# The combine of a mixture-of-experts layer: sums from accumulators, squares on ScalarE, a new order of the pass, four shared-expert groups early

## The chip, the cores and the metric

One Trainium2 chip, one core of it. The time is that of the whole kernel on the device in microseconds, a median over runs. "A change within measurement" means about 0.2% here.

## What is computed

An attention layer with random features, then a layer with 32 routed experts (four per token, at most 512 tokens each) and one shared expert; both are wrapped in `x + layernorm(f(layernorm(x)))`. The change touches the end of the second:

```python
ye = jnp.einsum('eci,eid->ecd', h, W2)                 # routed experts
yrows = ye[eid, posc] * gflat[:, None]
out = yrows.reshape(-1, K, D).sum(axis=1)
out = out + jax.nn.silu(X @ sw1.T) * (X @ sw3.T) @ sw2.T   # shared expert
x = x + _layernorm(out)          # (out - mean) / sqrt(var + 1e-5)
```

There are T = 8192 tokens of E = 512 numbers; float32 outside of the matmuls.

## The kernel before

Three stretches matter. First, routing ends: GpSimd scatters token slots to DRAM (`send`, L1260), one indirect DMA per 128 choices. Meanwhile the shared expert runs for NS = 2 groups *early* (`up`, `down`, `silu`, `make_high`, `hidden`, `low`, `copy_early`), and their result is stored to the accumulator `acc` in DRAM (`store_early`, L1564). Then slots are loaded, the rows of expert 0 gathered (L1412), turned on TensorE (`turn`, L1462) and the 32 experts run. Each adds its weighted rows to `acc` by an indirect DMA of GpSimd (L1426).

Last comes the combine, 16 passes `q` over the groups in ORDER. A *heavy* pass has a group whose shared expert was not early: it forms `up` of the next group and `down` of this one. A *light* pass (groups under NS) has no shared expert left. In each heavy pass:

- TensorE: `up` of the next group, 32 matmuls 128x512 (L1485), `down` of this one, 4 x 4 matmuls (L1500) into two banks `ys`, of which the third and fourth `down` wait until `include` has read the first and second.
- ScalarE: `silu` of the next group's two halves (L1540), `make_high` (L1546, the rounded half of `h`), `scale` of the pass before (L1552, four instructions with a scale and a bias per partition: the layernorm), `store` (L1559, a DMA issue).
- VectorE: `make_shift` (L1663, 128x4), `hidden` (L1610), `low` (L1615), `include` (L1642: `acc` block plus `ys`), `measure` (L1651, bn_stats of a block), `add` (L1670: the residual, 2048 wide), `aggregate` (L1656).
- GpSimd: `make_rstd`, variance plus epsilon (L1436) and its power -0.5 (L1438), between `aggregate` and `make_shift`.
- SP: `load_acc` (L1361; five buffers `total`), `load_shared` (L1348, the turned groups; eight buffers), `load_x1` (L1354; five buffers, a new load waits for the store that frees it).

A single `stats`, `mv`, `rstd` and `shift` serve all passes. ScalarE's table for silu is loaded once before the first `silu`.

## Time and profile before

| | us |
|---|---|
| median of 3 runs | 2089.63 (2088.13 to 2090.12) |
| the profiled execution, whole | 2089.07 |
| its span, first to last instruction | 2087.3 |
| TensorE busy | 1819.7 (87%) |
| VectorE busy | 1207.8 (58%) |
| ScalarE busy | 1124.8 (54%) |
| GpSimd busy | 758.3 (36%) |

All times within the trace are counted from the start of the span. Shares of the span are averages over stages with different limits, so the stretches have to be read one by one. The granted clock is TensorE's, as a share of full speed.

### The profile page before, as it was taken

What the parts mean: (1) busy time and instruction counts of PE and PEld (TensorE: products, weight loads), DVE (VectorE), ACT (ScalarE), POOL (GpSimd) and SP (SyncE); (2) the same over time, 40 slices, a digit from 0 to 9 for tenths busy, and PEclk for the clock granted to TensorE, in tenths of its full rate; (3) what the DMA queues carried; (4) which work ended last, traced back from release to release, by engine and by line L of the source; (5) the groups of instructions that cost most, each with busy time, mean ns of one, the idle gap of its engine ahead of it and who ended that gap; (6) DMA issues with size and microseconds to landing.
All of it is one profiled execution on the core that took longest, in us unless ns stands there. A gap on an engine that the chain in (4) does not pass through costs nothing.

```text
span 2087.3 us, 33721 instructions
## 1 busy us (share of the span) xinstructions
PE 1819.7 (87%) x12976; PEld 889.0 (43%) x12976; DVE 1207.8 (58%) x2230; ACT 1124.8 (54%) x1371; POOL 758.3 (36%) x718
## 2 busy tenths in 40 slices
PE   8999999999969998897888887455999989987795
PEld 5444444444448785132333333222444444443331
DVE  6776767676620000376888898861444344445786
ACT  5565555555436665586778775513444444432443
POOL 0000000000000000015877787874777777761110
PEclk9999999999979999999999999777999999999997
DMA  7445444446368885768877775342999999987983
GB/s 249 165 137 184 143 177 143 178 139 212 107 173 211 211 212 133 171 206 180 244 220 222 230 221 186 137 171 79 203 206 234 242 241 241 202 147 243 344 292 129
DMA packets 188848, 405.15 MB, mean 194 GB/s; under 512 B 33812, under 2 KB 72084, under 8 KB 172064
## 3 DMA queue, kind: packets, MB, share of 16 engines
q1 hardware_dynamic: 83184, 222.41, 35.6%
q10 hardware_dynamic: 68640, 124.26, 17.3%
q0 software_dynamic: 36864, 56.32, 14.4%
q8 instruction: 103, 1.69, 0.3%
q14 instruction: 57, 0.47, 0.1%
HBM read 237.06 MB, written 177.08 MB: 198 GB/s over the span
## 4 chain that ended last, share of the span: by engine, by line
PE 13%; DMA 12%; DVE 12%; issue 10%; POOL 9%; ACT 4%; SPq 1%; POOLq 0%; DVEq 0%; ACTq 0%
POOL slot_dram L1260 4%; DMA acc_dram<-s_y,s_slot 3%; PE s_gates L1485 3%; PE s_ups L1485 3%; PE s_ys L1500 2%; DMA s_spread<-share_dram 2%; DMA s_rows<-rows_dram,s_slot 2%; POOL acc_dram L1426 2%; DMA den_dram<-s_den 2%; PE s_turned L1462 1%; DVE s_stats L1651 1%; ACT s_xT L1531 1%; DVE s_x L1670 1%; POOL s_rows L1412 1%; PE s_y L898 1%
## 5 line engine op out<-in xcount | busy, mean ns | idle before, releaser
L258 PE MATMUL s_proj<-s_xT,keep_wqkv 128*128 128x512 f16 x1536 | 341.8, 379 | 0.0
L1260 POOL DMA_INDIRECT slot_dram<-keep_filled,keep_slots x256 | 292.1, 1141 | 105.2 <-issue 74.4
L1426 POOL DMA_INDIRECT acc_dram<-s_y,s_slot x128 | 205.1, 1603 | 93.0 <-issue 35.6
L258 PEld LDWEIGHTS s_proj<-s_xT,keep_wqkv 128*128 128x128 f16 x1536 | 147.8, 98 | 183.2 <-issue 12.6
L898 PE MATMUL s_y<-keep_wo,s_at_hl 128*128 128x512 f16 x768 | 188.6, 398 | 36.9 <-ACT s_z L988 36.9
L1540 ACT ACTIVATE s_gate<-s_gates 128x512 f32<-128x512 f32 x96 | 57.1, 597 | 263.8 <-PE s_ups L1485 218.4
L1610 DVE SCALAR_TENSOR_TENSOR s_h<-s_gate,s_ups 128x512 f32<-128x512 f32 x96 | 65.9, 686 | 216.1 <-ACT s_gate L1540 216.1
L339 POOL TENSOR_SCALAR s_rstd<-s_mv 128x4 f32<-128x4 f32 x16 | 16.0, 998 | 458.9 <-DVE s_mv L354 458.9
L676 ACT ACTIVATE s_phi<-s_logits 128x1024 f32<-128x1024 f32 x128 | 131.1, 1024 | 83.9 <-PE s_logits L697 83.9
L237 PE MATMUL s_proj<-keep_wqkv,s_xT 128*128 128x512 f16 x768 | 173.8, 383 | 1.2 <-ACT s_xT L500 1.2
L967 ACT ACTIVATE s_phi<-s_logits 128x1024 f32<-128x1024 f32 x128 | 131.4, 1027 | 63.5 <-PE s_logits L867 62.6
L518 ACT ACTIVATE s_hl<-s_rot 128x1024 f16<-128x1024 f32 x64 | 67.6, 1057 | 179.0 <-DVE s_rot L400 169.9
L387 DVE TENSOR_TENSOR s_by_cos<-s_proj,s_table 128x1024 f32<-128x1024 f32 x64 | 78.3, 1224 | 133.6 <-PE s_proj L258 133.6
L1531 ACT ACTIVATE s_xT<-s_turned 128x1024 f16<-128x1024 f16 x128 | 125.5, 1019 | 44.5 <-PE s_turned L1462 44.2
L1412 POOL DMA_INDIRECT s_rows<-rows_dram,s_slot x128 | 132.7, 1037 | 42.7 <-issue 30.8
L898 PEld LDWEIGHTS s_y<-keep_wo,s_at_hl 128*128 128x128 f16 x768 | 72.7, 101 | 170.6 <-issue 55.7
L737 PE MATMUL s_parts<-s_phi,s_v 128*33 128x128 f32 x2048 | 137.9, 277 | 2.3 <-DMA s_v<-v_dram 2.2
L1500 PE MATMUL s_ys<-s_w,s_parts 128*128 128x512 bf16 x512 | 132.1, 382 | 3.5 <-DVE s_y L1627 3.5
L1485 PE MATMUL s_gates<-s_xT,s_w 128*128 128x512 f16 x512 | 124.3, 387 | 10.4 <-ACT s_xT L1531 10.4
L1485 PE MATMUL s_ups<-s_xT,s_w 128*128 128x512 f16 x512 | 122.1, 382 | 0.0
L1627 DVE TENSOR_SCALAR s_y<-s_ys,s_slot 128x512 f32<-128x512 f32 x128 | 93.9, 748 | 43.8 <-PE s_ys L1500 43.6
L1462 PE MATMUL s_turned<-keep_ident,s_rows 128*128 128x128 f16 x1024 | 80.3, 223 | 44.6 <-DMA s_rows<-rows_dram,s_slot 35.0
(165 smaller groups left out, 3202.8 us busy)
## 6 DMA issues: line engine op xcount, KB each, us to landing
s_x<-x_in SPq DMA_DIRECT2D x32, 1024.0 KB, 11.9
qk_dram<-s_hl ACTq DMA_DIRECT2D x32, 1024.0 KB, 6.0
keep_ahead<-qk_dram SPq DMA_DIRECT2D x48, 512.0 KB
acc_dram<-s_zero SPq DMA_DIRECT2D x17, 1024.0 KB, 13.9
v_dram<-s_v ACTq DMA_DIRECT2D x16, 1056.0 KB, 6.9
s_v<-v_dram SPq DMA_DIRECT2D x16, 1056.0 KB, 11.2
s_spread<-share_dram SPq DMA_DIRECT2D x64, 256.0 KB
x_dram<-s_x ACTq DMA_DIRECT2D x16, 1024.0 KB, 5.6
```

The lines of the kernel that those rows point to most:

```text
L237: mm = nc.tensor.matmul(proj[half][:, 512 * b:512 * b + 512], left, right, start=(c == 0 and i == 0), stop=(c == EC - 1 and i == 2))
L258: mm = nc.tensor.matmul(out[:, 512 * b:512 * b + 512], left, right, start=(c == 0 and i == 0), stop=(c == EC - 1 and i == 2))
L676: nc.scalar.activation(phi[n % 2][:].rearrange("p h m -> p (h m)"), logits[n % 2][:], ACT.Exp, scale=1.0 / M_SCALE).then_inc(phi_ready, 1)
L737: mm = nc.tensor.matmul(parts[ch % 2][at:at + D + 1, h // 2 * M:(h // 2 + 1) * M], v[n % 2][:, a * H + h, :], phi[half][:, h % HALF, :], s ...
L898: mm = nc.tensor.matmul(y[m % 2][:], at_hl[n % 2][:, s, c, a * P:(a + 1) * P], keep["wo"][:, w, c, :], start=(c == 0 and i == 0), stop=(c ...
L967: nc.scalar.activation(phi[m % PHIS][:].rearrange("p h q -> p (h q)"), logits[:], ACT.Exp, scale=1.0 / M_SCALE).then_inc(phi_ready, 1)
L1260: nc.gpsimd.indirect_dma_start(out=io["slot"], out_offset=bass.IndirectOffsetOnAxis(ap=slots[n % 2][:, a * K + j:a * K + j + 1], axis=0), ...
L1412: nc.gpsimd.indirect_dma_start(out=rows[r][:, a, :], out_offset=None, in_=io["rows"], in_offset=bass.IndirectOffsetOnAxis(ap=slot[e % RING ...
L1426: nc.gpsimd.indirect_dma_start(out=io["acc"], out_offset=bass.IndirectOffsetOnAxis(ap=slot[e % RING][:, a, 0:1], axis=0), in_=y[e % 2][:, ...
L1485: mm = nc.tensor.matmul(bank[:], w[:, c, i * P:(i + 1) * P], left[:, s, c, :], start=(c == 0 and s == 0), stop=(c == EC - 1 and s == 1))
L1500: mm = nc.tensor.matmul(ys[a % 2][:], parts[p % 2][:, i, s, a * P:(a + 1) * P], w[:, i, :], start=(i == 0 and s == 0), stop=(i == IC - 1 a ...
L1531: nc.scalar.activation(xT[k][:, :, :, a * P:(a + 1) * P], turned[a % 2][:].bitcast(F16).rearrange("p (s c q) -> p s c q", s=2, c=EC), ACT. ...
```

## The change

NS becomes 4: four shared-expert groups run early, and four of the combine's passes are light. `include` writes out the sum of each row with its result (`accum_out`), so `measure` and `aggregate` go; in a light pass `sum_up` does it, adding a tile of zeros that a memset sets once. `center` makes minus the mean, scaled; ScalarE's `square` forms the sum of the squares of the centred block, which is the variance. The small tiles become pairs, so that passes wait two back instead of one. ScalarE's order in a pass is now `square`, `silu` 0, `make_high` 0, `store` of two passes back, `scale`, `silu` 1, `make_high` 1. VectorE's is `hidden` 0, `make_shift`, `low` 0, `include` 0 and 1, `hidden` 1, `include` 2 and 3, `center`, `low` 1, `add`.

```diff
-        NS = 2
+        NS = 4
-        ORDER = (2, 3, 4, 0, 5, 6, 7, 1, 8, 9, 10, 11, 12, 13, 14, 15)
+        ORDER = (4, 5, 0, 6, 7, 1, 8, 9, 2, 10, 11, 3, 12, 13, 14, 15)
...
+        sums, centre, var, rstd, shift = (t.pair(n, [P, A]) for n in ("sums", "centre", "var", "rstd", "shift"))
+        squares = xT[0][:].rearrange("p s c q -> p (s c q)").bitcast(F32).rearrange("p (a e) -> p a e", a=A)
+        nothing = w13[0][:].rearrange("p w c i -> p (w c i)").bitcast(F32)[:, 0:E]
...
+            def make_rstd(q):
+                k = q % 2
+                pool.wait_ge(squared, q + 1)
+                if q >= 2:
+                    pool.wait_ge(z_ready, q - 1)
+                nc.gpsimd.tensor_scalar(rstd[k][:], var[k][:], 1e-5, None, ALU.add).then_inc(var_ready, 1)
...
+            def square(q):
+                k = q % 2
+                act.wait_ge(centre_ready, q + 1)
+                for a in range(A):
+                    ins = nc.scalar.activation(squares[:, a, :], total[q % ACCS][:, a, :], ACT.Square,
+                                               bias=centre[k][:, a:a + 1], scale=E ** -0.5,
+                                               accum_out=var[k][:, a:a + 1])
+                ins.then_inc(squared, 1)
...
+                if q >= 1:
+                    square(q - 1)
                 if more:
-                    for i in range(IC):
-                        silu(p + 1, i)
+                    silu(p + 1, 0)
                     make_high(p + 1, 0)
+                if q >= 2:
+                    store(q - 2)
                 if q >= 1:
                     scale(q - 1)
                 if more:
+                    silu(p + 1, 1)
                     make_high(p + 1, 1)
-                if q >= 1:
-                    store(q - 1)
+            square(NG - 1)
+            store(NG - 2)
             scale(NG - 1)
             store(NG - 1)
...
                 nc.vector.scalar_tensor_tensor(out=at, in0=ys[a % 2][:], scalar=1.0 / H_SCALE, in1=at, op0=ALU.mult,
-                                               op1=ALU.add).then_inc(y_copied, 1)
+                                               op1=ALU.add, accum_out=sums[q % 2][:, a:a + 1]).then_inc(y_copied, 1)
+
+            def sum_up(q, a):
...
+                nc.vector.scalar_tensor_tensor(out=at, in0=at, scalar=1.0, in1=nothing, op0=ALU.mult, op1=ALU.add,
+                                               accum_out=sums[q % 2][:, a:a + 1]).then_inc(summed, 1)
+
+            def center(q):
...
+                nc.vector.tensor_scalar(centre[k][:], sums[k][:], -E ** -1.5, None, ALU.mult).then_inc(centre_ready, 1)
...
+            nc.vector.memset(nothing, 0.0).then_inc(nothing_set, 1)
+            dve.wait_ge(nothing_set, 1)
             for q, n in enumerate(ORDER):
                 p = NE + n
+                more = n >= NS and p + 1 < PASSES
+                if more:
+                    hidden(p + 1, 0)
                 if q >= 1:
                     make_shift(q - 1)
+                if more:
+                    low(p + 1, 0)
                 if n >= NS:
...
                     include(q, 0)
+                    include(q, 1)
                     if more:
                         hidden(p + 1, 1)
...
                     include(q, 2)
...
                     include(q, 3)
...
+                        sum_up(q, a)
+                center(q)
+                if more:
+                    low(p + 1, 1)
+                if q >= 1:
                     add(q - 1)
-                aggregate(q)
             make_shift(NG - 1)
             add(NG - 1)
```

## Rows read from the trace of the kernel before

**Rows 1.** The page: busy us (share of the span) and instructions of each engine.
```profile
PE 1819.7 (87%) x12976; PEld 889.0 (43%) x12976; DVE 1207.8 (58%) x2230; ACT 1124.8 (54%) x1371; POOL 758.3 (36%) x718
```

**Rows 2.** Busy time by stretch: us, then PE, PEld, DVE, ACT, POOL, PEclk, DMA, GB/s.
```profile
1898.00:2087.00 189.00, 142.65 (x600) 57.96 (x600) 147.57 (x267) 73.76 (x113) 20.23 (x32) 0.88 0.73 265
...
1932.00:1952.00 20.00, 12.79 (x53) 5.13 (x52) 15.36 (x32) 8.58 (x13) 3.40 (x6) 0.83 0.99 369
```

**Rows 3.** Timeline of a heavy pass: start, us, engine, line, operation, count, [idle before, releaser].
```profile
2042.14 0.16 DVE L1663 SCALAR_TENSOR_TENSOR s_shift<-s_mv,s_rstd 128x4 f32<-128x4 f32 x1 [1.47 <-POOL s_rstd L1438]
2042.25 0.69 DVE L1610 SCALAR_TENSOR_TENSOR s_h<-s_gate,s_ups 128x512 f32<-128x512 f32 x1
2042.86 0.68 DVE L1642 SCALAR_TENSOR_TENSOR s_rows<-s_ys,s_rows 128x512 f32<-128x512 f32 x1
2042.97 0.63 ACT L1546 ACTIVATE s_parts<-s_h 128x512 f16<-128x512 f32 x1 [0.46 <-DVE s_h L1610]
...
2043.51 2.92 ACT L1552 ACTIVATE s_rows<-s_rows,s_shift,s_rstd 128x512 f32<-128x512 f32 x4
...
2048.83 2.28 DVE L1670 TENSOR_TENSOR s_x<-s_x,s_rows 128x2048 f32<-128x2048 f32 x1
...
2051.14 0.38 ACTq L1559 DMA_DIRECT2D out_dram<-s_x  x1
...
2051.62 0.60 ACT L1540 ACTIVATE s_gate<-s_gates 128x512 f32<-128x512 f32 x1 [4.68 <-DVE s_x L1670]
2051.75 0.38 DVE L1656 BATCH_NORM_AGGREGATE s_mv<-s_stats 128x2 f32<-128x6 f32 x4
...
2053.60 0.16 DVE L1663 SCALAR_TENSOR_TENSOR s_shift<-s_mv,s_rstd 128x4 f32<-128x4 f32 x1 [1.47 <-POOL s_rstd L1438]
```

**Rows 4.** Timeline of a light pass and of TensorE's first matmuls behind it.
```profile
1975.96 0.16 DVE L1663 SCALAR_TENSOR_TENSOR s_shift<-s_mv,s_rstd 128x4 f32<-128x4 f32 x1 [1.47 <-POOL s_rstd L1438]
...
1983.18 0.16 DVE L1663 SCALAR_TENSOR_TENSOR s_shift<-s_mv,s_rstd 128x4 f32<-128x4 f32 x1 [1.47 <-POOL s_rstd L1438]
...
1984.63 3.67 PE L1500 MATMUL s_ys<-s_sw,s_parts 128*128 128x512 bf16 x8 [7.21 <-DVE s_rows L1642]
```

**Rows 5.** Timeline of the combine's first two passes, and the last shift.
```profile
1898.22 0.69 DVE L1642 SCALAR_TENSOR_TENSOR s_y<-s_ys,s_y 128x512 f32<-128x512 f32 x1 [12.87 <-DMA s_y<-acc_dram]
...
1911.55 0.69 DVE L1642 SCALAR_TENSOR_TENSOR s_y<-s_ys,s_y 128x512 f32<-128x512 f32 x1 [3.07 <-PE s_ys L1500]
...
1922.29 0.16 DVE L1663 SCALAR_TENSOR_TENSOR s_shift<-s_mv,s_rstd 128x4 f32<-128x4 f32 x1 [1.47 <-POOL s_rstd L1438]
...
2074.96 0.16 DVE L1663 SCALAR_TENSOR_TENSOR s_shift<-s_mv,s_rstd 128x4 f32<-128x4 f32 x1 [1.47 <-POOL s_rstd L1438]
```

**Rows 6.** Timeline of TensorE between the routing and the first expert.
```profile
1397.50 1.89 PE L1500 MATMUL s_ys<-s_sw,s_parts 128*128 128x512 bf16 x8
...
1401.07 5.62 PE L1500 MATMUL s_ys<-s_sw,s_parts 128*128 128x512 bf16 x24 [1.67 <-DVE s_y L1635]
...
1425.66 1.89 PE L1462 MATMUL s_turned<-keep_ident,s_rows 128*128 128x128 f16 x16 [18.97 <-DMA s_rows<-rows_dram,s_slot]
```

**Rows 7.** ScalarE's instructions by line: busy us, mean ns, idle us before, releasers.
```profile
L522 ACT ACTIVATE s_sq<-s_rot 128x1024 f32<-128x1024 f32 x64 | 66.6, 1040 | 0.0
...
L1546 ACT ACTIVATE s_parts<-s_h 128x512 f16<-128x512 f32 x96 | 60.2, 627 | 69.0 <-DVE s_h L1610 69.0
...
L1552 ACT ACTIVATE s_rows<-s_rows,s_shift,s_rstd 128x512 f32<-128x512 f32 x36 | 26.3, 801 | 13.7 <-DVE s_shift L1663 13.7
...
L1018 ACT ACTIVATE s_grown<-s_route 128x128 f32<-128x128 f32 x16 | 4.4, 278 | 37.0 <-DVE keep_slots L1195 33.5 <-PE s_route L924 3.4
...
L1540 ACT ACT_TABLE_LOAD x1 | 1.3, 1283 | 23.7 <-PE s_ups L1485 23.7
```

**Rows 8.** The chain that ended last, in two successive experts: start, us, what.
```profile
1474.03 1.90 PE s_gates L1485 x8
...
1487.17 1.90 PE s_gates L1485 x8
```

More of the change, by code:

```diff
@@ L1314, in expert_and_combine_programs @@
             "p (a e) -> p a e", a=A) for r in rows]
[L1315 to L1316 removed]
+        sums, centre, var, rstd, shift = (t.pair(n, [P, A]) for n in ("sums", "centre", "var", "rstd", "shift"))
+        power = t.sb("power", [P, A])
+        squares = xT[0][:].rearrange("p s c q -> p (s c q)").bitcast(F32).rearrange("p (a e) -> p a e", a=A)
+        nothing = w13[0][:].rearrange("p w c i -> p (w c i)").bitcast(F32)[:, 0:E]
         turned = [t.psum(f"turned{b}") for b in range(2)]
@@ L1449, in pool_program @@
                 pool.wait_ge(added[k], 16 * A * NE // 2)
-            for n in range(NG):
-                make_rstd(n)
+            for q in range(NG):
+                make_rstd(q)
         def pe_program(pe):
@@ L1546, in make_high @@
                 nc.scalar.activation(parts[e % 2][:, i, 0, :], h[i][:], ACT.Copy).then_inc(high_ready, 1)
+            def square(q):
[6 more added lines that the diff above has]
+                ins.then_inc(squared, 1)
             def scale(q):
                 act.wait_ge(shift_ready, q + 1)
-                at = total[q % ACCS]
+                at, k = total[q % ACCS], q % 2
                 for a in range(A):
-                    ins = nc.scalar.activation(at[:, a, :], at[:, a, :], ACT.Identity, bias=shift[:, a:a + 1],
-                                               scale=rstd[:, a:a + 1])
+                    ins = nc.scalar.activation(at[:, a, :], at[:, a, :], ACT.Identity, bias=shift[k][:, a:a + 1],
+                                               scale=rstd[k][:, a:a + 1])
                 ins.then_inc(z_ready, 1)
@@ L1642, in include @@
                 nc.vector.scalar_tensor_tensor(out=at, in0=ys[a % 2][:], scalar=1.0 / H_SCALE, in1=at, op0=ALU.mult,
-                                               op1=ALU.add).then_inc(y_copied, 1)
-            def measure(q, a):
-                n = ORDER[q]
+                                               op1=ALU.add, accum_out=sums[q % 2][:, a:a + 1]).then_inc(y_copied, 1)
+            def sum_up(q, a):
+                at = total[q % ACCS][:, a, :]
+                dve.wait_ge(acc_loaded[q % ACCS], 16 * (q // ACCS) + 16)
+                nc.vector.scalar_tensor_tensor(out=at, in0=at, scalar=1.0, in1=nothing, op0=ALU.mult, op1=ALU.add,
+                                               accum_out=sums[q % 2][:, a:a + 1]).then_inc(summed, 1)
+            def center(q):
+                n, k = ORDER[q], q % 2
                 if n >= NS:
-                    dve.wait_ge(y_copied, A * (NE + n) + a + 1)
+                    dve.wait_ge(y_copied, A * (NE + n) + A)
                 else:
-                    dve.wait_ge(acc_loaded[q % ACCS], 16 * (q // ACCS) + 16)
-                nc.vector.bn_stats(stats[:, a, :], total[q % ACCS][:, a, :]).then_inc(stats_ready, 1)
-            def aggregate(q):
-                dve.wait_ge(stats_ready, A * (q + 1))
-                for a in range(A):
-                    ins = nc.vector.bn_aggr(mv[:, a, :], stats[:, a, :])
-                ins.then_inc(mv_ready, 1)
+                    dve.wait_ge(summed, A * (len([m for m in ORDER[:q] if m < NS]) + 1))
+                nc.vector.tensor_scalar(centre[k][:], sums[k][:], -E ** -1.5, None, ALU.mult).then_inc(centre_ready, 1)
             def make_shift(q):
+                k = q % 2
                 dve.wait_ge(rstd_ready, q + 1)
-                if q >= 1:
-                    dve.wait_ge(z_ready, q)
-                nc.vector.scalar_tensor_tensor(out=shift[:], in0=mv[:, :, 0], scalar=-1.0, in1=rstd[:], op0=ALU.mult,
+                if q >= 2:
+                    dve.wait_ge(z_ready, q - 1)
+                nc.vector.scalar_tensor_tensor(out=shift[k][:], in0=sums[k][:], scalar=-1.0 / E, in1=rstd[k][:], op0=ALU.mult,
                                                op1=ALU.mult).then_inc(shift_ready, 1)
```

33 lines of the change are left out of this document (6 added, 27 removed).

## The prediction, made before the change was run

> **What bounds the kernel now.** I read the page's busy shares first: TensorE 87% of the span, no other engine over 58% [rows 1]. That is an average, so the second view is the busy time by stretch: the change touches two, the gap before the experts and the combine. In the combine TensorE is busy 142.65 of 189 us and VectorE 147.57 of 189 [rows 2]: VectorE leads.
>
> The timeline of one combine pass says why [rows 3]. The shift of one pass starts at 2042.14 and that of the next at 2053.60: 11.46 us a pass. VectorE runs 512-wide instructions 0.60 us apart (2042.25 to 2042.86), twelve a pass, then the 2048-wide add (2.28, of which the last 0.08 overlaps its successor, as the shift does) and four aggregates (0.38), and then stands 1.47 us for GpSimd's two instructions. 12 x 0.60 + 2.20 + 0.38 + 0.10 + the waits of 1.47 and some 0.1 is 11.4: the pass is one closed ring on VectorE and nothing else is in it. TensorE needs 48 matmuls of 0.216 (8 in 1.89 of which 0.16 is pipeline behind the last [rows 6]): 10.4 us.
>
> A pass without shared expert (a light pass) takes 7.22 us (1975.96 to 1983.18), and TensorE starts cold behind it: the granted clock of a stretch with a light pass is 0.83 of 2.4 GHz [rows 2], so part of it ran at 1.2, and 8 matmuls take 3.67 instead of about 1.9 [rows 4]. The combine begins when the first accumulator block lands at 1898.22; the first two passes end with the shift at 1922.29, and the last shift starts at 2074.96 [rows 5]. What follows (scales, add, store) the change leaves alone.
>
> At the gap before the experts TensorE waits for gathered rows, which come late because GpSimd still scatters slots: it stands 18.97 us and turns the first rows at 1425.66. The two early groups lie in that shadow; their last matmul ends about 1406.5 (1401.07 + 5.62 less 0.16 of pipeline) [rows 6].
>
> **The combine after, part by part.** *VectorE* loses per heavy pass four bn_stats (4 x 0.60) and four aggregates (0.38) and gains a centre instruction of the kind of the shift (128x4, 0.16, next after 0.10) and the reading of four sums. It then holds 8 x 0.60 + 2.20 + 0.20 = 7.2 us plus those reads: it is the bound no more. *ScalarE* gains four squares. Its own rows [rows 7]: a 512-wide ACTIVATE with no per-partition operand takes 0.627, with two (scale and bias) 0.801, so with one, as in a square, 0.71; the four scales of a pass take 2.92 [rows 3], so follow each other by 0.705, and squares by 0.61.
>
> The reading of a sum is in no row. Lower end 0 (nothing is removed, so no gain). Upper end on ScalarE the smallest ACTIVATE that it runs, 0.28 [rows 7]; on VectorE a 128x4 instruction that must await the end of its forerunner, 0.16 + 0.09 = 0.25 (0.69 long, successor after 0.60) [rows 3]. Aggregates follow each other by 0.09, which pulls to the low side. I take 0.15 on ScalarE and 0.10 on VectorE. The Trainium skill (*VectorE: DVE Perf Modes*, section on two Vector instructions with no wait between them) says that an operation that writes out its accumulator is two instructions; no row here shows it.
>
> The new order makes another ring, through both engines. From the start of one centre to that of the next, with 0.04 for each hand-over (2042.25 + 0.69 to 2042.97 in rows 3): centre 0.20; squares 4 x 0.76 = 3.04; silu 0 0.64; hidden 0 0.73; high 0 0.54 (2042.97 to 2043.51); issue of the store 0.48 (issued 2051.14, ScalarE's next instruction at 2051.62); scales 2.82; silu 1 0.64; hidden 1 0.60; include 2 0.70; include 3 0.83: **11.22 us**. The 1.47 of GpSimd goes: the shift is ready 5.0 after the centre, and ScalarE reaches the scales only at 5.6. What is late next is ScalarE. Include 2 and 3 queue on VectorE behind hidden 1, that behind silu 1, that behind the scales. So the pass gains 0.24, not the 4 us by which VectorE is relieved. TensorE's ring, 48 matmuls and 0.17 for a bank, is 10.55; it recovers only 0.65 a pass from the cold start behind a light pass, so passes there come to about 11.5.
>
> A light pass after: shift 0.10; four sum_up 4 x 0.70 + 0.13; centre 0.20; squares 3.04 + 0.10; GpSimd 1.47: 7.84, against 7.22.
>
> Laid end to end from the landing of the first block to the shift of the last pass: first two passes 22.0 (as before, the cold TensorE brings the second group's first output to VectorE at 1911.55 [rows 5]; then four includes and a hidden 4.1, squares 3.1, GpSimd 1.5: 1920.2, 24.07 before), four light 31.2, eight heavy of 11.54 around them 92.3, one of 11.2, the last 10.2 (no next group, but its downs wait for banks): 166.9. Before: 2074.96 - 1898.22 = 176.7. **Gain 9.8 us.** About 7 of it is two passes that became light; the rest is the start and the passes behind light ones. At no cost: the memset (VectorE waits 12.9 for the first block anyway [rows 5]; without that cover half a microsecond), and the store a pass later. That one stands before the scales with its output long ready; behind it on SP are an x1 load (lands some 20 us before its add) and the next accumulator load, four passes ahead. Traffic in the combine falls by 2 MB (two turned groups fewer to load).
>
> **The gap before the experts.** Two more groups are 2 x 48 matmuls early, with two more loads, two more stores of 1 MB (ScalarE's queue, before its first turn copy) and eight copies. An early group costs the two-bank stop too: up 6.92, then down 0 and 1 1.73, stop to 1401.07, down 2 and 3, 5.3 from the first down at 1397.50 to the end of the fourth at 1402.8: 12.2 a group. So TensorE ends at 1406.5 + 24.4 = 1430.9 instead of the 1425.66 at which it is wanted, and ScalarE issues the last store before its first copy (0.4): **+5.6 us**. The shadow was 19 us, the two groups take 24.4. The shift is carried on: the experts pass it through gates 13.14 apart (1474.03 to 1487.17), with nothing idle between for long [rows 8]. Bounds: a TensorE that is warm in the experts' first two ups, where it is now cold behind its waits, would give back up to 1.8 (3.67 less 1.89 [rows 4, 6]) for each, and 0.4 in the turns, so 4; a first pass that is cold again, or stores that meet the gathers, costs up to 3 more. So +1.6 to +8.6; I take 5.6, for the ends are about equally far.
>
> **Sum.** The profiled execution lasted 2089.07 us (span 2087.3), 0.56 under the median of 2089.63. 2089.07 - 9.8 + 5.6 = 2084.9, as a median 2085.4; rounded, 2085.
>
> **The rivals.** (1) *Sums read for nearly nothing* (0.05 each on both engines): ScalarE's ring falls to 10.7, near TensorE's 10.55; end to end the combine gains 18: 2089.6 - 18 + 5.6 = 2077; at zero 2074. For it: aggregates 0.09 apart. Against: a sum is complete only when its instruction is. (2) *Slower, by the price of the sums*: each 0.05 on ScalarE costs 4 x 16 x 0.05 = 3.2 us and, with what TensorE then waits, about 4; each 0.05 on VectorE about 2. From 0.20 and 0.15 on the combine no longer pays for the gap (gain 6); at 0.30 and 0.20 the gain is 1 and the time 2089.6 - 1 + 5.6 = 2094. (3) *Squares and silus need different tables.* A table load takes 1.28 [rows 7]. With Square outside silu's set, eleven heavy passes with a next group pay two each: 22 x 1.28 = 28 us on the ring: 2085 + 28 = 2113. Against: the lines show one load before the first silu, while L522's 64 squares ran among copies with none of their own [rows 7]; but that is another set. The Trainium skill (*ScalarE: Activation LUTs*, Table sets) names relu, copy, identity and abs as in every set, not square; no row shows silu's set with a square. (4) *Loads become the bound.* A light pass moves 3.15 MB in 7.8 us, 404 GB/s, above the 369 of a full stretch [rows 2]. Over three passes with one light it is 9.4 MB and a turned group of 1.05 in 31 us, 340 GB/s, and buffers hold five blocks; so what decides is only whether a light pass waits for its own 3.15 MB: at 369 GB/s 8.5 us instead of 7.8, four times, 2088. (5) *The early groups stay hidden after all* (the gathers later, the clock warm): 2081; the change gives what it says.
>
> **Chances.** Forecast, 2080 to 2090: 0.64, with (5) in it; (1) 0.17; (2) 0.12; (3) 0.03; (4) 0.04. The range leaves out 0.03 of (3), half of (2) beyond 2094 and what is under 2073: 2073 to 2094. A measurement of this kernel tells about 0.2% (4.2 us) from no change: faster means under 2085.4, slower over 2093.8. The forecast lies on that edge: half of its 0.64 counts as faster, with (1) 0.49; slower is half of (2), (3) and 0.04 for an expert stage that shifts more than I see, 0.13; same is the rest, 0.38.
>
> **What would show it.** Right: heavy passes of 11.2 to 11.6 between shifts, light ones of 7.8; VectorE idle before hidden 1, released by ScalarE; ScalarE without a gap from centre to silu 1; TensorE's first turn of rows at 1431, directly behind a down; no table load beyond the two. Wrong: passes of 10.6 (the sums are cheap, TensorE bounds), over 11.8 (dear), the first turn still at 1426, waits for loads in the combine, or an expert stage that takes up the delay in waits of its own.

## The result and the profile after

The changed kernel takes 2073.72 us (median of 4 runs, 2071.74 to 2075.23). The kernel before, run beside it, takes 2089.88 (4 runs). The ratio is 0.9917, with a 95% interval of 0.9896 to 0.9939: 16.2 us less, where 4.5 were forecast. The direction was right and the time lies in the range, near its lower end, but the gain is 3.6 times what the sum gave.

The profiled execution lasted 2071.74 us (span 2069.9). First the page's busy line, which answers [rows 1]: VectorE fell by 27.5 us, ScalarE rose by 45.1, TensorE and the number of its matmuls are what they were.

```profile
PE 1821.6 (88%) x12976; PEld 890.0 (43%) x12976; DVE 1180.3 (57%) x2199; ACT 1169.9 (57%) x1499; POOL 758.9 (37%) x718
```

Since neither engine that gained or lost is near 100%, this says little. The span has to be cut at places that both traces have: the first early matmul (begin), the first turn of gathered rows, the first matmul of the experts, the first include of the combine, and the last shift. Times in us:

| stretch | before | after | difference |
|---|---|---|---|
| start to first early matmul | 1381.70 | 1379.14 | -2.56 |
| first early matmul to first turn of rows (the gap) | 43.96 | 48.97 | +5.01 |
| first expert matmul to first include | 467.35 | 467.36 | 0.0 |
| first include to last shift (the combine) | 176.74 | 156.76 | -19.98 |
| last shift to end | 12.34 | 12.51 | +0.17 |

With 0.05 less between the first turn and the first expert matmul (5.16 for 5.21) these add up to the 17.4 by which the spans differ. The first row is code that the change leaves alone. Over all kernels of this study, in which neither that code nor the experts' matmuls were touched, the first early matmul began between 1373.9 and 1384.8 and the expert stage took 464.9 to 478.1; that it is equal to 0.01 here is chance. So a whole time of one execution can be off by several us, and what follows compares stretches; whole times are given as medians, with their intervals where there are several runs. A stretch has its own scatter: four kernels with the changed kernel's combine, instruction for instruction (this one and three of experiment 8), took 156.76, 156.90, 157.69 and 158.14 for it. A difference under 1.4 us in the combine of one trace says nothing.

The combine in the view of busy time by stretch (columns: window, its length, then PE, PEld, DVE, ACT, POOL busy with their counts, PEclk, DMA share, GB/s):

```profile
1901.00:2070.00 169.00, 122.11 (x504) 50.48 (x504) 109.14 (x218) 115.33 (x233) 20.26 (x32) 0.85 0.79 283
1940.00:2000.00 60.00, 47.98 (x203) 20.12 (x201) 41.79 (x83) 45.37 (x92) 7.59 (x12) 0.89 0.93 327
```

In [rows 2] VectorE led with 147.57 of 189; now TensorE leads with 122.11 of 169, and nobody is at 100%. One heavy pass in the timeline (start, us, engine, line, operation, count, idle before and its releaser) answers [rows 3]:

```profile
2022.11 0.17 DVE L1673 TENSOR_SCALAR s_centre<-s_sums 128x4 f32<-128x4 f32 x1
2022.31 0.72 ACT L1555 ACTIVATE s_xT<-s_rows,s_centre 128x512 f32<-128x512 f32 x1 [1.04 <-DVE s_centre L1673]
2022.94 0.19 ACT L1555 ACTIVATION_READ_ACCUMULATOR s_xT<-s_rows,s_centre 128x1 f32 x1
2023.03 0.71 ACT L1555 ACTIVATE s_xT<-s_rows,s_centre 128x512 f32<-128x512 f32 x1
...
2025.15 0.57 ACT L1543 ACTIVATE s_gate<-s_gates 128x512 f32<-128x512 f32 x1
2025.75 0.69 DVE L1626 SCALAR_TENSOR_TENSOR s_h<-s_gate,s_ups 128x512 f32<-128x512 f32 x1 [0.69 <-ACT s_gate L1543]
2026.48 0.63 ACT L1549 ACTIVATE s_parts<-s_h 128x512 f16<-128x512 f32 x1 [0.76 <-DVE s_h L1626]
2026.48 0.38 ACTq L1571 DMA_DIRECT2D out_dram<-s_x  x1
...
2027.01 2.91 ACT L1564 ACTIVATE s_rows<-s_rows,s_shift,s_rstd 128x512 f32<-128x512 f32 x4
...
2029.83 0.57 ACT L1543 ACTIVATE s_gate<-s_gates 128x512 f32<-128x512 f32 x1
2030.00 0.69 DVE L1658 SCALAR_TENSOR_TENSOR s_rows<-s_ys,s_rows 128x512 f32<-128x512 f32 x1 [0.16 <-PE s_ys L1503]
...
2030.62 0.68 DVE L1626 SCALAR_TENSOR_TENSOR s_h<-s_gate,s_ups 128x512 f32<-128x512 f32 x1
2031.39 0.69 DVE L1658 SCALAR_TENSOR_TENSOR s_rows<-s_ys,s_rows 128x512 f32<-128x512 f32 x1
2032.01 0.69 DVE L1658 SCALAR_TENSOR_TENSOR s_rows<-s_ys,s_rows 128x512 f32<-128x512 f32 x1
...
2032.74 0.17 DVE L1673 TENSOR_SCALAR s_centre<-s_sums 128x4 f32<-128x4 f32 x1
```

From centre to centre it is 10.63 us, where 11.46 stood before and 11.22 was forecast. Three things are to be seen. A sum is an instruction of its own on ScalarE, 0.19 long, but the next square starts 0.09 after it: squares are 0.72 apart here, 0.71 in the mean, not 0.76. Two includes with their sums are 0.62 apart (2031.39, 2032.01), not 0.70. And the store's issue (2026.48) runs beside the ACTIVATE of the same start; the scales follow 0.53 later, as in [rows 3], where nothing was issued there. An include between silu 1 and hidden 1 waits 0.16 for TensorE, so the ring through ScalarE isn't what ends last in this pass.

A light pass, and the matmuls behind it, for [rows 4]:

```profile
2008.77 0.16 DVE L1680 SCALAR_TENSOR_TENSOR s_shift<-s_sums,s_rstd 128x4 f32<-128x4 f32 x1 [1.64 <-POOL s_rstd L1441]
2008.97 2.93 ACT L1564 ACTIVATE s_y<-s_y,s_shift,s_rstd 128x512 f32<-128x512 f32 x4 [1.67 <-DVE s_shift L1680]
2011.42 0.17 DVE L1673 TENSOR_SCALAR s_centre<-s_sums 128x4 f32<-128x4 f32 x1
2011.81 0.70 ACT L1555 ACTIVATE s_xT<-s_y,s_centre 128x512 f32<-128x512 f32 x1
...
2016.19 0.16 DVE L1680 SCALAR_TENSOR_TENSOR s_shift<-s_sums,s_rstd 128x4 f32<-128x4 f32 x1 [0.27 <-POOL s_rstd L1441]
...
2017.97 3.29 PE L1503 MATMUL s_ys<-s_sw,s_parts 128*128 128x512 bf16 x8 [6.01 <-DVE s_rows L1658]
```

It takes 7.42 (2008.77 to 2016.19), and its ring goes through ScalarE: ScalarE waits 1.67 for the shift, scales for 2.84, and its squares start right behind (2011.81), with the centre ready since 2011.59.

The four starts behind light passes are not alike. The first eight matmuls took 3.60, 3.34, 3.60 and 3.29, and the granted clock over the first 5.8 to 5.9 us was 0.54, 0.75, 0.56 and 0.76. Where it was the lower, the eight matmuls behind them took 2.87 and 2.77 instead of 1.89, and the two heavy passes lie 1.24 and 1.13 over twice 10.53; where it was the higher, 0.04 and 0.09. So a cold start cost about 1.2 us or nothing, in the same code.

The start and the end of the combine, for [rows 5]:

```profile
1900.63 0.69 DVE L1658 SCALAR_TENSOR_TENSOR s_y<-s_ys,s_y 128x512 f32<-128x512 f32 x1 [10.84 <-DMA s_y<-acc_dram]
...
1920.92 0.16 DVE L1680 SCALAR_TENSOR_TENSOR s_shift<-s_sums,s_rstd 128x4 f32<-128x4 f32 x1 [1.64 <-POOL s_rstd L1441]
...
2057.39 0.16 DVE L1680 SCALAR_TENSOR_TENSOR s_shift<-s_sums,s_rstd 128x4 f32<-128x4 f32 x1 [2.23 <-POOL s_rstd L1441]
```

And the gap, TensorE and what it waits for, for [rows 6]:

```profile
1399.91 1.89 PE L1488 MATMUL s_gates<-s_shared_xT,s_sw 128*128 128x512 f16 x8
...
1412.11 1.89 PE L1488 MATMUL s_gates<-s_shared_xT,s_sw 128*128 128x512 f16 x8
...
1422.58 5.69 PE L1503 MATMUL s_ys<-s_sw,s_parts 128*128 128x512 bf16 x24 [1.67 <-DVE s_y L1651]
...
1428.11 1.06 PE L1465 MATMUL s_turned<-keep_ident,s_rows 128*128 128x128 f16 x16
```

A group is 12.20 apart (1399.91 to 1412.11), and the first turn comes directly behind the last down, with no idle time: the 18.97 of before are used up.

### The profile page after: what moved, and what is told of

It is laid out like the page before. It is cut to its first block, busy times and chain, and to the rows that moved or that the text cites. A ratio compares the mean times of both kernels' runs of the same rounds, so it can differ in the third digit from the quotient of the medians.

```text
span 2069.9 us, 33813 instructions
## 1 busy us (share of the span) xinstructions
PE 1821.6 (88%) x12976; PEld 890.0 (43%) x12976; DVE 1180.3 (57%) x2199; ACT 1169.9 (57%) x1499; POOL 758.9 (37%) x718
## 4 chain that ended last, share of the span: by engine, by line
PE 17%; DMA 13%; DVE 10%; issue 8%; ACT 6%; POOL 5%; SPq 1%; POOLq 0%; DVEq 0%; ACTq 0%
PE s_gates L1488 5%; PE s_ups L1488 4%; PE s_ys L1503 4%; DMA s_spread<-share_dram 4%; DMA acc_dram<-s_y,s_slot 3%; DMA den_dram<-s_den 2%; DMA s_rows<-rows_dram,s_slot 2%; POOL slot_dram L1260 2%; POOL acc_dram L1428 2%; ACT s_xT L1534 1%; ACT s_xT L1555 1%; PE s_turned L1465 1%; PE s_y L898 1%; DMA share_dram<-s_share 1%; ACT s_phi L967 1%
## 5 line engine op out<-in xcount | busy, mean ns | idle before, releaser
L1488 PE MATMUL s_gates<-s_xT,s_w 128*128 128x512 f16 x512 | 124.0, 386 | 13.3 <-ACT s_xT L1534 10.6
L237 PEld LDWEIGHTS s_proj<-keep_wqkv,s_xT 128*128 128x128 f16 x768 | 75.1, 99 | 90.5 <-issue 3.9
```

The source lines that it names most:

```text
L237: mm = nc.tensor.matmul(proj[half][:, 512 * b:512 * b + 512], left, right, start=(c == 0 and i == 0), stop=(c == EC - 1 and i == 2))
L1488: mm = nc.tensor.matmul(bank[:], w[:, c, i * P:(i + 1) * P], left[:, s, c, :], start=(c == 0 and s == 0), stop=(c == EC - 1 and s == 1))
```

## The experiments

T1 is the theory that the sums are cheap and TensorE bounds the steady heavy pass; T2 is the prediction's own, that ScalarE's ring does.

**1. Two early groups with the new pass.**

```diff
-        NS = 4
+        NS = 2
...
-        ORDER = (4, 5, 0, 6, 7, 1, 8, 9, 2, 10, 11, 3, 12, 13, 14, 15)
+        ORDER = (2, 3, 4, 0, 5, 6, 7, 1, 8, 9, 10, 11, 12, 13, 14, 15)
```

> The changed kernel with two early groups instead of four (NS = 2 and the order of before), all else as changed. Stretch A is from the first include to the last shift (before 176.7 us, changed 156.8). Theory 1, TensorE's 48 matmuls bound a heavy pass at 10.5 and a light pass takes 7.4: two heavy passes more, two light ones and two cold starts less, so A is 161 to 162; the gap before the experts gives back its 4.9 (TensorE turns the first rows when they land, not behind a down). In all 2073.7 + 4.5 - 4.9, no difference that can be told from the changed kernel (2071 to 2076). Theory 2, ScalarE's ring bounds (the prediction's 11.2 less the cheaper sums, 10.8): A near 165 and the whole 2077.

The combine took 160.96 us and the gap 43.50; steady heavy passes were 10.53, as T1 has it. The whole time is 2071.47 (ratio to before 0.9921, 0.9897 to 0.9946; the changed kernel has 0.9917). So the new pass alone, with the groups of before, gives 15.8 of the 20 us of the combine, and the whole gain within what can be told. Two more early groups take another 4.2 from the combine and put 5.5 on the gap: as far as these stretches tell, they give nothing.

**2. The old pass with four early groups.** The opposite half, made from the kernel before.

```diff
-        NS = 2
+        NS = 4
...
-        ORDER = (2, 3, 4, 0, 5, 6, 7, 1, 8, 9, 10, 11, 12, 13, 14, 15)
+        ORDER = (4, 5, 0, 6, 7, 1, 8, 9, 2, 10, 11, 3, 12, 13, 14, 15)
```

> The kernel before with NS = 4 and the changed order of groups, nothing else. Both theories: a pass stays at 11.46, two become light at 7.2, which is 8.5 us less, and two more cold starts give 2 to 3 back, so stretch A is 170 to 172 instead of 176.7; the gap costs 4.9. In all 2089.9 - 5.5 + 4.9 = 2089, no difference from before. If it comes to 2084 or less, the early groups carry more of the 16 us than the rewritten pass does.

Combine 167.61, gap 49.45, whole 2080.59 (ratio 0.9968, 0.9948 to 0.9988). By its whole time this kernel meets the sign that was set for early groups that carry more than the pass: 2080.59, and 6.5 less than the kernel before beside it (2087.06). The stretches don't bear that out (9.1 off the combine, 5.5 on the gap, 3.6 in all), and experiment 1 has nearly the whole gain without these groups. The expectation was too dear on the cold starts. Behind a light pass the first heavy pass took 11.45, as any other, and the second 12.08 to 12.28, so each cold start costs 0.6 to 0.8; before, the two cost 0.6 and 1.7. So the same two groups give 9.1 us in the old pass (two times 11.46 - 7.21 = 8.5, and 0.6 in the first and last pass and the cold starts), and in the new one 4.2: two times 10.53 - 7.42 = 6.2, and 0.5 in the first two passes, less 1.1 for more cold starts and less 1.4 in the last pass (9.61 where two early groups have 8.18). Where that 1.4 comes from was not settled.

**3. Squares without their sums.**

```diff
-                                               bias=centre[k][:, a:a + 1], scale=E ** -0.5,
-                                               accum_out=var[k][:, a:a + 1])
+                                               bias=centre[k][:, a:a + 1], scale=E ** -0.5)
...
+            for k in range(2):
+                nc.vector.memset(var[k][:], 1.0).then_inc(nothing_set, 1)
```

> The changed kernel whose squares write out no sum; the variance is a constant 1, so this part of the result is left out. It prices ScalarE's sums: squares should follow each other by 0.61 instead of 0.71. Theory 1 (TensorE bounds the steady pass): steady heavy passes stay at 10.5, light ones fall from 7.4 to 7.0, the heavy ones around them by up to 0.4; A 153 to 154. Theory 2 (ScalarE bounds): all passes fall by 0.4, A 150.

```profile
2008.73 2.55 ACT L1555 ACTIVATE s_xT<-s_y,s_centre 128x512 f32<-128x512 f32 x4
2011.18 0.58 ACT L1543 ACTIVATE s_gate<-s_gates 128x512 f32<-128x512 f32 x1
```

This is the timeline of ScalarE: four squares and the next silu, 2.45 from start to start, 0.61 each, where four with sums take 2.84. A sum on ScalarE costs 0.10. The combine went to 152.34, 4.4 less: 0.36 in each light pass (7.06), 1.8 in the last pass (7.81 for 9.61), 0.7 in the first two and 0.4 in the nine heavy passes together, where T2 asks 0.39 of each, 3.5 in all. The whole took 2067.56 (one run). T1 expected 153 to 154 and T2 150, so the sum lies nearer to T1; that the heavy passes stay says that they don't follow ScalarE.

**4. Includes without their sums.**

```diff
-                                               op1=ALU.add, accum_out=sums[q % 2][:, a:a + 1]).then_inc(y_copied, 1)
+                                               op1=ALU.add).then_inc(y_copied, 1)
...
-                nc.vector.scalar_tensor_tensor(out=at, in0=at, scalar=1.0, in1=nothing, op0=ALU.mult, op1=ALU.add,
-                                               accum_out=sums[q % 2][:, a:a + 1]).then_inc(summed, 1)
+                nc.vector.scalar_tensor_tensor(out=at, in0=at, scalar=1.0, in1=nothing, op0=ALU.mult, op1=ALU.add
+                                               ).then_inc(summed, 1)
```

> The changed kernel whose include and sum_up write out no sum; the mean is a constant 0, so this part of the result is left out. Price by the trace of the changed kernel 0.01 each (0.61 after 0.60): A 156 to 157, no change. With the prediction's 0.10 it would fall by 4 us to 153.

Combine 157.55 against 156.76, whole 2072.77 (one run): no change. Since TensorE bounds the heavy pass, that alone would not price the sums; the distances do. Without sums, four sum_ups last 2.49 in all, 0.60 apart, where they are 0.61 or 0.62 with them. The sums that VectorE takes along are nearly free. In the lines of the changed kernel (group | busy, mean ns | idle before, releaser) the three prices stand together:

```profile
L1555 ACT ACTIVATE s_xT<-s_rows,s_centre 128x512 f32<-128x512 f32 x36 | 25.5, 710 | 7.3 <-DVE s_centre L1673 7.3
...
L1555 ACT ACTIVATION_READ_ACCUMULATOR s_xT<-s_rows,s_centre 128x1 f32 x36 | 6.7, 187 | 0.0
...
L1658 DVE DVE_READ_ACCUMULATOR s_rows<-s_ys,s_rows 128x1 f32 x28 | 2.3, 83 | 0.0
```

**5. Dear sums: each square in two halves, each with a sum.** The opposite of 3: four more ACTIVATEs of 256 columns and four more reads on ScalarE a pass.

```diff
-                    ins = nc.scalar.activation(squares[:, a, :], total[q % ACCS][:, a, :], ACT.Square,
+                    nc.scalar.activation(squares[:, a, E // 2:], total[q % ACCS][:, a, E // 2:], ACT.Square,
+                                         bias=centre[k][:, a:a + 1], scale=E ** -0.5,
+                                         accum_out=var2[k][:, a:a + 1])
+                    ins = nc.scalar.activation(squares[:, a, :E // 2], total[q % ACCS][:, a, :E // 2], ACT.Square,
```

> The changed kernel with each square made in two halves of 256, each with its sum (the variance takes one half only, so half of it is left out). It adds four fixed costs and four sums to ScalarE's pass, 0.28 each: 1.1 us. Theory 1: ScalarE's ring (about 10.0 us without a wait for TensorE) grows to 11.1 and takes over from TensorE's 10.5: heavy passes 11.1 to 11.5, light 8.5, A 168 to 171. Theory 2: A 156.8 + 16 x 1.1 = 174.

```profile
2001.25 0.50 ACT L1556 ACTIVATE s_xT<-s_rows,s_centre 128x256 f32<-128x256 f32 x1
2001.65 0.19 ACT L1556 ACTIVATION_READ_ACCUMULATOR s_xT<-s_rows,s_centre 128x1 f32 x1
2001.74 0.49 ACT L1559 ACTIVATE s_xT<-s_rows,s_centre 128x256 f32<-128x256 f32 x1
```

Halves are 0.49 apart, so eight take 3.93 for 2.84: 1.09 more a pass. Light passes took 8.53 (all of it: 1.11 more), the nine heavy ones behind the first two passes 11.38 to 11.94, the combine 172.25 (15.5 more), the whole 2098.8 (one run). That lies between T1's 168 to 171 and T2's 174 and doesn't separate them by itself. The waits do: VectorE now stands 0.94 before hidden 1, for ScalarE's silu. This is the prediction's mechanism: with 1.1 us more, ScalarE's ring does bound the heavy pass. In the changed kernel it lies close below TensorE, at 11.38 - 1.09 = 10.29 for 10.53.

**6. The light passes last.** Whether the pass is TensorE's can be read only where no cold start disturbs it, so all heavy passes were put together.

```diff
-        ORDER = (4, 5, 0, 6, 7, 1, 8, 9, 2, 10, 11, 3, 12, 13, 14, 15)
+        ORDER = (4, 5, 6, 7, 8, 9, 10, 11, 12, 13, 14, 15, 0, 1, 2, 3)
```

> The changed kernel with the four light passes at the end of the order (heavy ones 4 to 15, then 0 to 3). Theory 1: TensorE never stops among the heavy passes, so they all take 10.5 and no cold start is paid; the last pass is a light one of 7.4 instead of 9.6. Stretch A falls from 156.8 to 150 or 151, the whole to 2068. Theory 2 (ScalarE bounds): 10.8 a pass and A near 154. Against both: the four last passes move 3.15 MB each in 7.4 us, 425 GB/s, so waits for loads there, up to 1 us a pass, and a later end of the last store.

Busy time by stretch, columns as above, and the timeline's shifts of a heavy and of a light pass:

```profile
1940.00:2000.00 60.00, 59.73 (x270) 25.75 (x273) 45.18 (x87) 45.38 (x92) 6.32 (x10) 1.00 0.85 295
```

```profile
1991.24 0.16 DVE L1680 SCALAR_TENSOR_TENSOR s_shift<-s_sums,s_rstd 128x4 f32<-128x4 f32 x1 [0.27 <-POOL s_rstd L1441]
...
2001.77 0.16 DVE L1680 SCALAR_TENSOR_TENSOR s_shift<-s_sums,s_rstd 128x4 f32<-128x4 f32 x1 [0.27 <-POOL s_rstd L1441]
...
2046.70 0.16 DVE L1680 SCALAR_TENSOR_TENSOR s_shift<-s_sums,s_rstd 128x4 f32<-128x4 f32 x1 [1.96 <-POOL s_rstd L1441]
...
2054.12 0.16 DVE L1680 SCALAR_TENSOR_TENSOR s_shift<-s_sums,s_rstd 128x4 f32<-128x4 f32 x1 [1.96 <-POOL s_rstd L1441]
```

TensorE is busy 59.73 of 60 us at a granted clock of 1.00, and nine passes in a row took 10.53 or 10.54: its 48 matmuls and a bank, within 0.02 the 10.55 of the prediction. The combine took 153.85, 2.9 less than in the changed order. The sum is near the 154 of T2, but not for its reason: T2 asked for passes of 10.8. T1 expected 150 to 151 because it gave up the last heavy pass of 9.6; that pass only stands elsewhere, and took 9.04. The 2.9 are what the changed kernel's heavy passes behind light ones lie over 10.53 (0.51 + 0.73 + 0.04 + 0.41 + 0.72 = 2.4) and this 0.57. Four light passes in a row took 7.42 each with no wait for a load, so transfers don't bound them. The whole time did not show it (2073.91, ratio 0.992, 0.9893 to 0.9947). The profiled execution (2075.89) reached the first early matmul at 1384.77, 5.6 later than that of the changed kernel; of the three other runs there is no trace.

**7. The store in its own pass.**

```diff
-                if q >= 2:
-                    store(q - 2)
                 if q >= 1:
                     scale(q - 1)
...
                     make_high(p + 1, 1)
-            square(NG - 1)
-            store(NG - 2)
+                if q >= 1:
+                    store(q - 1)
+            square(NG - 1)
```

> The changed kernel with the store where it was: at the end of ScalarE's pass, for the pass before. It waits there for VectorE's add, which ends about 2.8 us after the centre, and the squares queue behind it. Both theories: heavy passes 12.5 to 13.3 and light ones 9 to 10 instead of 10.5 and 7.4; stretch A (first include to last shift) 185 to 200 instead of 156.8, slower than before. If A stays near 157, the later store did nothing.

```profile
1995.02 0.17 DVE L1672 TENSOR_SCALAR s_centre<-s_sums 128x4 f32<-128x4 f32 x1
...
1995.70 2.28 DVE L1686 TENSOR_TENSOR s_x<-s_x,s_y 128x2048 f32<-128x2048 f32 x1
...
1998.02 0.46 ACTq L1571 DMA_DIRECT2D out_dram<-s_x  x1
1998.52 0.72 ACT L1555 ACTIVATE s_xT<-s_rows,s_centre 128x512 f32<-128x512 f32 x1 [4.09 <-DVE s_x L1686]
```

The squares, ready at 1995.2, start at 1998.52 behind a store that waits for the 2.28 us add. Heavy passes took 13.49 to 14.13 and light ones 10.31 to 10.38, both more than expected; the combine took 201.44, 44.7 more. The whole is 2119.4, and the kernel before beside it 2097.42 (one run each). Once the squares are on ScalarE, the place of one DMA issue is worth more than all that the change gains.

**8. What holds up the gap.** Four kernels. In the first VectorE frees a bank before it makes the last low part (the wait of 1.67 at 1422.58 above).

```diff
-                    for i in range(IC):
-                        hidden(p + 1, i)
-                        low(p + 1, i)
-                copy_early(p)
+                    hidden(p + 1, 0)
+                    low(p + 1, 0)
+                    hidden(p + 1, 1)
+                    copy_early(p, (0, 1))
+                    low(p + 1, 1)
+                    copy_early(p, (2, 3))
+                else:
+                    copy_early(p)
```

> The changed kernel; only VectorE's order in the early groups differs: hidden 1, copies 0 and 1, then low 1, copies 2 and 3. TensorE then stands about 0.3 us per group for a bank instead of 1.67, so its last early matmul ends 4 us sooner. If the early groups are all that TensorE is late by, the first turn of rows and everything behind come 1.5 to 4 us sooner (2070 to 2072); the upper figure if the gathered rows are there, the lower one if they land at 1426 to 1427 because the slot load meets a store of the early groups. If nothing moves, the gathers were the late one after all.

The gap stayed at 48.70 (48.97), the combine took 157.69 and the whole 2072.26 (ratio 0.9916, 0.9891 to 0.9941). TensorE did end 3.4 sooner (48.70 - 3.12 = 45.58 after its first early matmul), and then stood for rows:

```profile
1423.69 1.80 PE L1465 MATMUL s_turned<-keep_ident,s_rows 128*128 128x128 f16 x16 [3.12 <-DMA s_rows<-rows_dram,s_slot]
```

The chain that ended last goes through the last scatter of slots and the fourth gather, the last for which the first turn waits; here, and then in the kernel with two early groups (start, us, what):

```profile
1406.27 5.01 DMA slot_dram<-keep_filled,keep_slots
...
1417.69 5.95 DMA s_rows<-rows_dram,s_slot
```

```profile
1406.71 2.08 DMA slot_dram<-keep_filled,keep_slots
...
1415.39 3.44 DMA s_rows<-rows_dram,s_slot
```

The last scatter takes 5.01 instead of 2.08 and the gather 5.95 instead of 3.44. What is there in addition is the early groups' stores of 1 MB (one was issued at 1406.65, two from 1417.47 on). Three early groups tell the two causes apart, since TensorE's own work then ends long before the rows come:

```diff
-        NS = 4
+        NS = 3
...
-        ORDER = (4, 5, 0, 6, 7, 1, 8, 9, 2, 10, 11, 3, 12, 13, 14, 15)
+        ORDER = (3, 4, 5, 0, 6, 7, 8, 1, 9, 10, 11, 2, 12, 13, 14, 15)
...
-                        pool.wait_ge(y_stored[k], 16 * NS // 2)
+                        pool.wait_ge(y_stored[k], 16 * ((NS + 1 - k) // 2))
```

> The changed kernel with three early groups and three light passes. Gap G is from the first early matmul to the first turn of gathered rows (before 43.96 us, two early 43.50, four early 48.97, four early with sooner copies 48.70). Theory TensorE (it is the late one): three groups end 12.2 sooner than four, G falls to 43.9. Theory stores (an early group's 1 MB store delays the last scatter's landing, the slot load or the gathers): the second group's store is issued 34 us after the first early matmul as in the changed kernel, just where the last scatter lands, so G stays at 46 to 48. Stretch A 156.8 + 3.1 less one cold start = 159. The whole 2071 to 2074, not told from the changed kernel.

```profile
1424.02 1.89 PE L1465 MATMUL s_turned<-keep_ident,s_rows 128*128 128x128 f16 x16 [8.70 <-DMA s_rows<-rows_dram,s_slot]
```

The gap took 46.10, with TensorE idle for 8.70: TensorE's own part ends 37.4 after its first matmul (46.10 - 8.70), and yet the rows come 2.6 later than with two groups (43.50, with TensorE idle for 18.89). The rows are late by themselves. Of the 2.6, 0.9 is GpSimd's, which began its last scatter later (32.20 after the first early matmul for 31.34). This time the scatter took 2.09 and it was the load of the slots that was slow, 5.44 instead of 1.74, with two early stores issued beside it at 1412.29. The combine took 160.04 and the whole 2074.64 (ratio 0.9937, 0.9912 to 0.9962). That the stores delay the rows is argued so far. So next the stores were put behind the gathers (early results kept in the tiles of x1, all four stored after the second turn), without and with the order of the first kernel:

```diff
-                              y[p % 2][:]).then_inc(y_stored[p % 2], 16)
+                              x1[p][:]).then_inc(y_stored[p % 2], 16)
...
-                if p >= 1:
-                    store_early(p - 1)
-            store_early(NS - 1)
...
             turn(1)
+            for p in range(NS):
+                store_early(p)
...
-                    nc.vector.tensor_scalar(y[p % 2][:, a, :], ys[a % 2][:], 1.0 / H_SCALE, None,
+                    nc.vector.tensor_scalar(x1[p][:, a, :], ys[a % 2][:], 1.0 / H_SCALE, None,
```

> The changed kernel; the early groups' results wait in the x1 tiles, free until expert 18, and all four stores are issued after ScalarE's second turn of rows. Nothing meets the last scatters, the slot load or the first gathers, but TensorE still works on the early groups. G stays at 48.5 to 49.0 (TensorE), the rows lie ready before it; G 44 would mean that TensorE's end was not late at all.

> Both: the late stores, and VectorE's copies of blocks 0 and 1 ahead of low 1. TensorE ends 4 sooner and no store meets the gathers. If both are late at once in the changed kernel, which is why neither alone gained, G falls to 44.0 to 45.0, and all behind comes 4 to 5 us sooner: near 2069. If G stays at 48, a third thing is late.

Late stores alone: 48.77, nothing (combine 156.90, whole 2073.15 in one run). Both together: 45.66. The timeline of TensorE in the second:

```profile
1417.65 5.62 PE L1506 MATMUL s_ys<-s_sw,s_parts 128*128 128x512 bf16 x24 [0.29 <-DVE s_x L1649]
1423.11 1.06 PE L1468 MATMUL s_turned<-keep_ident,s_rows 128*128 128x128 f16 x16
```

The stop for a bank is 0.29 instead of 1.67, and the turn follows without idle time. Only the stores, and the tiles that hold their data until then, tell this kernel from the first of the four: there the fourth gather was issued 42.70 after the first early matmul and the rows were waited for, here it is 40.31 (40.02 with two groups) and they are not. Two things were late at the same time, TensorE and the rows; either one mended alone leaves the other, at the same 48.7. The combine took 158.14, within its scatter, and the whole time is 2066.81 (ratio 0.9908, 0.9877 to 0.994).

**9. All of it, light passes last.** The kernel with late stores and early copies, with the order of experiment 6.

> As the run with both, and the light passes last. G 44 to 45, stretch A 153.9 as with the light passes last alone: 4.5 and 2.9 less than the changed kernel, 2066 to 2067, a ratio to before of 0.990 or less.

Gap 45.36, combine 154.54, whole 2067.03 (0.9913, 0.9889 to 0.9936). Against the changed kernel the two stretches give 3.6 and 2.2 us. The two kernels can't be told from each other by their whole times, and their ratios to the kernel before (2084.36 here) overlap that of the changed kernel. Late stores alone, on the same chip, took six more, but that is no evidence: it is one run, and its expert stage took 474.72 where theirs took 468.34 and 467.09. That they are faster than the changed kernel rests on the stretches alone; the whole times don't show it.

## Why the prediction was right in sign and wrong in size

The forecast was 11.3 us too high. The combine holds 10.1 of it: 156.76 for 166.9. Laid against the prediction's own list, from its landing of the first block to its last shift:

| part | forecast | measured |
|---|---|---|
| first two passes | 22.0 | 20.3 |
| four light passes | 31.2 | 29.7 |
| nine heavy passes | 103.5 | 97.2 |
| the last pass | 10.2 | 9.6 |

**The heavy pass: mechanism named, size wrong, and with it the bound.** "What is late next is ScalarE" is the step that failed. The ring that the prediction laid is there, instruction for instruction, but three of its terms were too dear. The read of a sum on ScalarE was taken at 0.15 and adds 0.10 (four squares 2.84 instead of 3.04; experiment 3). On VectorE it was taken at 0.10 and adds 0.01: the two includes and the centre behind them take 1.35 instead of 1.53. The issue of the store was put at 0.48 and costs nothing in the rows (0.53 to the next ACTIVATE with it, 0.54 without). 11.22 - 0.20 - 0.18 - 0.48 = 10.36, which is under TensorE's 10.55. Two runs agree: experiment 5 gives 10.29, and in experiment 6 hidden 1 starts 0.79 behind silu 1 instead of the 0.61 of experiment 5, because the include before it waits for TensorE; 10.53 less 0.18 is 10.35. Neither the sums alone (10.84) nor the store alone (10.74) would have changed the bound; together they do, and the pass stops at TensorE's 10.53 (experiment 6). The 0.48 was read where ScalarE stood for the add and nothing ran beside the issue: the price of a row holds for the state in which it was taken. Four light passes of 7.84 are 31.4, not 31.2; that changes nothing.

**The price of a sum.** The bounds 0 to 0.28 and 0 to 0.25 held the truth; within them the nearest row, aggregates 0.09 apart, was named and then not followed. What it did not reckon with is overlap: an instruction that reads the accumulator is 0.19 long here and costs half of that, since its successor starts 0.10 before its end. The Trainium skill (*ScalarE: Activation LUTs*, What ACT_TABLE_LOAD costs) gives back-to-back ACTIVATEs an overlap of about 93 ns; the trace agrees, with squares 0.71 long and, without sums, 0.61 apart. What the Trainium skill says of VectorE in the sentence that the prediction cites, that an operation which writes out its accumulator is two instructions, the trace shows too: 0.69 and a read of 0.083. But most of the read lies in the tail of the main instruction (2029.14 + 0.69 = 2029.83, the read from 2029.76 to 2029.84).

**The light pass** was a ring through VectorE's four sum_ups and the centre: 7.84. Those run beside the scales of the pass before and are ready 0.2 before them; what is left is ScalarE's scales of 2.84, its squares of 2.91 to the end of the last read, and its wait of 1.67: 7.42.

**The first two passes and the cold starts.** TensorE's first 8 matmuls behind a light pass took 3.29 to 3.60, not the 3.67 of [rows 4], and heavy passes behind light ones 10.5 to 11.3 instead of 11.5. The granted clock of the stretch from 1940 to 2000 is 0.89, and of heavy passes alone (experiment 6) 1.00, so the cold start is there, but in all it costs the 2.4 us worked out under experiment 6, nearly all of it behind two of the four light passes. Of the 1.7 in the first two passes, 1.1 is the cold start too: the second group's first include came 12.19 behind the first one (1900.63 to 1912.82), where the prediction kept the 13.33 of [rows 5]. TensorE's first gates there, before and after:

```profile
1902.44 2.96 PE L1485 MATMUL s_gates<-s_shared_xT,s_sw 128*128 128x512 f16 x8
```

```profile
1904.78 1.89 PE L1488 MATMUL s_gates<-s_shared_xT,s_sw 128*128 128x512 f16 x8
```

That part is luck: other kernels with this pass took up to 21.5 for these two passes. The other 0.6 are the cheaper squares and includes, whose parts no run told apart.

**The gap was right**: +5.0 for +5.6, groups 12.2 apart as worked out, the first turn directly behind a down, and the store's issue ahead of the first turn copy. It is carried through the experts (467.36 for 467.35), though no closer than their scatter of several us allows one to say. Right for one reason too few, though: stores do meet scatter and gather (experiment 8), which was counted only as a bound of up to 3, and was hidden by TensorE's being as late.

**"About 7 of it is two passes that became light"** held for neither pass: 9.1 with the old (experiment 2), 4.2 with the new (experiment 1). The new pass, which the prediction gave about 3 us, brings 15.8.

**The rivals.** (1), nearly free sums at 2077, with 0.17, came nearest: its combine gain of 18 stands against 20 measured. But its condition, 0.05 on both engines, held on VectorE only; ScalarE's sums cost 0.10, and what made up for it are the free issue of the store and the shorter cold starts, which no rival named. So its figure is in part luck. (2), dear sums, fell; experiment 5 shows what more work on ScalarE would have done. Its own sums don't come out either: at its prices of 4 and 2 us a step the gain at 0.20 and 0.15 is 9.8 - 6 = 3.8, not 6, and at 0.30 and 0.20 it is a loss of about 6, not a gain of 1. (3), a table load in each turn from square to silu, fell: with all squares among the silus the profile has one load at the first silu, as in [rows 7]:

```profile
L561 ACT ACT_TABLE_LOAD x1 | 1.3, 1283 | 0.7 <-PEq L1878 0.7
...
L1543 ACT ACT_TABLE_LOAD x1 | 1.3, 1283 | 23.3 <-PE s_ups L1488 23.3
```

(4), loads as the bound, fell: light passes of 7.42 in a row had no wait for a load (experiment 6). (5), early groups that stay hidden, fell with the gap.

**What was named to watch for** worked: "passes of 10.6 (the sums are cheap, TensorE bounds)" is what the trace shows, with the store's issue as the other half of the reason.

## What to carry to other kernels

Before a new bound is declared, hold the laid-out ring against the next engine's own minimum: here 11.22 stood 0.67 over 10.55, less than the doubt in its terms, so the two cases deserved nearly equal chances. Read the price of a DMA issue or of a small read where it runs beside other work, not where its engine stands still. Where a gap doesn't shrink when its last cause is mended, look for a second one that ends at the same time, and mend both in one kernel.

## What the runs showed of the hardware

A sum by accumulator costs a 128x512 ACTIVATE 0.10 us of distance to its successor (0.71 in the changed kernel, 0.61 without sums in experiment 3) and a 128x512 scalar_tensor_tensor 0.01 or 0.02 (0.61 or 0.62, and 0.60 in experiment 4). A DMA issue on ScalarE's queue whose wait is long fulfilled runs beside an ACTIVATE and adds nothing (scales 0.53 behind it, 0.54 without it before). Where its wait is open it holds everything behind it: in experiment 7 ScalarE stood 4.09, 3.3 of it with the squares ready. With stores of 1 MB under way, in the first kernel of experiment 8, the last scatter of slots landed after 5.01 us instead of 2.08 with two early groups, and the fourth gather after 5.95 instead of 3.44; with three groups the scatter was as quick as ever (2.09) and the load of the slots took 5.44 instead of 1.74. Square and silu ran in alternation, 64 squares in all, with no table load between them. Behind a light pass, in which TensorE stood for 6.0 us, its granted clock over the next 5.8 to 5.9 us was 0.54 to 0.56 two times and 0.75 to 0.76 two times, in one execution of the same code.
